# Another order for the first tiles of a fused conv, scan and FFN kernel: one load queue, half of the first u between two v stages, the third x split earlier

## The chip, the cores and the metric

The kernel runs on 1 core of a Trainium2 chip. The metric is the device time of the program in microseconds, as the median of several runs. The engines are TensorE (PE), VectorE (DVE), ScalarE (ACT), GpSimd (POOL) and SyncE (SP, which here only issues DMAs). Each runs its own list of instructions in the order written, and they wait for each other on semaphores.

## The reference

The input x has 8192 rows (tokens) of 512 numbers. Cut to what matters:

```python
def attn(x):                       # called with layernorm(x)
    u, v = split(x @ in_proj_w + in_proj_b, 2)      # 512 -> 2 x 512
    v = conv3_depthwise(silu(v)) + conv_b           # along the tokens
    h_t = a * h_(t-1) + ssm_b * v_t                 # a = sigmoid(logit_a); a scan over the tokens
    y = ssm_c * h + ssm_d * v
    out = (u * silu(y)) @ out_proj_w + out_proj_b
    return layernorm(out + x) * ln_w + ln_b
def ffn(x):                        # called with layernorm(x)
    h = gelu(x @ ternary(W1).T + b1)                # 512 -> 2048
    return h @ ternary(W2).T + b2                   # 2048 -> 512
# ternary(w) = clip(round(w / mean|w|), -1, 1): the threshold needs the whole of w
x = x + layernorm(attn(layernorm(x)))
x = x + layernorm(ffn(layernorm(x)))
```

## The kernel before

The tokens are cut into 16 tiles of 512 (TT), each as four blocks of 128 rows (j) and, transposed, as four blocks of 128 features (b). The stages of a tile are:

- **front**: layer norm statistics of x on DVE (`ln1`: `x_stats`, `aggr`), 1/sqrt on POOL (`rstd_x`), the normed x on ACT (`norm_x`), and its split into two 16-bit halves, `t_hi` on ACT and `t_lo` on DVE, in one of four buffers `tp`. SP then issues one DMA transpose for each block j into `x1T` (`transposes("t1", t)`).
- **v** and **u** (`in_proj`): 12 matmuls of 128x512 for each b. v goes through `silu_v` on ACT, the three conv taps (`centre_tap` on ACT, `taps` first and second on DVE, with the edge column of the next tile copied by POOL), `d_conv` on ACT, `scan` and `y` on DVE, `silu_y` on ACT. `gate` (DVE) multiplies by u; `gate_hi` (ACT) and `gate_lo` (DVE) split the result.
- **o**: the output projection, 48 matmuls, then on DVE `h_add`, `h_stats` and `norms`: `a1`, `a2`, statistics, `x1`, statistics, `n3`, with three 1/sqrt on POOL between them (`rstd`, `rstd_b`, `rstd`). `t_hi` and `t_lo` split the result for the transposes into `x3T` ("t3").
- **f1** and **f2**: 16 blocks j each of 8 matmuls a tile. A block of f1 goes through `gelu` and `hi` on ACT and `lo` on DVE; f2 follows LAG = 4 blocks behind.

The weights are prepared ahead of the tiles. in_proj is scaled by a power of two found from its largest entry and split (`split_in` on ACT, `setup_split` on DVE); out_proj is split too (`split_out`, `setup_out_proj`). For the ternary weights |W1| and |W2| are summed (`abs_sum`, four quarters each, on ACT or DVE), the sum goes across the partitions by a small matmul (`threshold(0)` for W1, `threshold(1)` for W2), and then each weight is turned into -1, 0, 1 by a `sign` on ACT and a `ternary` on DVE, by chunks in the list ORDER. `w_ok` counts the finished chunks. Chunks 16 and up are loaded a second time (`reload(o)`), and their buffers come free as ternaries end: `reload(16)` waits for chunk 12, and so on. `w_ok` 4 releases the first f1, `w_ok` 8 the first gelu (its buffers held raw W1), `w_ok` 12 the first `lo`.

PSUM has eight banks: `misc` 0 and 1 for u, v and o, `f1b` 0 and 1 for f1, `f2b` 0 to 3 for the sums of f2. In the first tiles, where f1 and f2 haven't begun, all eight serve v, u and o (`bank`). From step 2 on `take` lets a group have its `misc` bank when the reader of the group two places ahead in the list `groups` is done: `gate` for a u, `silu_v` for a v, `h_add` for an o.

The order of work of the first tiles is written out by hand on every engine. On TensorE it is v(0), v(1), threshold(0), u(0), the output projection of tile 0 (`o_first`, which takes block k as soon as `gate_lo(0, k)` is done), v(2) with threshold(1) inside it. Then come the steps s = 2, 3, ...: step s does f1 and f2 of tile s-2, u and o of tile s-1 and v of tile s+1. In step 2 nine blocks of f1 come first, with f2 four behind, then u(1), four blocks of f2, o(1), half of v(3), the rest of f1. On DVE, ACT and POOL a step's items are sorted by hand-set times (`AT_...`), and step 2's list for DVE holds the scans and gates of tile 1, the `lo` of the first nine blocks and ternaries 12 to 20 (`AT_TERNARY`). `warm(n)` issues n matmuls of 128x128 in fp32, two instructions each, whose result nobody reads.

SP's order is: x tile 0, in_proj, x tile 1, the transposes of tile 0, the row vectors, out_proj, the transposes of tile 1, x tile 2, W1 quarter 2, W2, the transposes of tile 2, those of x3 of tile 0, then the reloads. W1 quarters 0, 1 and 3 are issued by ACT, after in_proj's third quarter has landed.

## Time and profile before

| | us |
|---|---|
| time before, median of 3 runs | 1496.58 (1496.28 to 1498.77) |
| the profiled execution, its own time | 1500.86 |
| its span | 1498.8 |
| TensorE busy in it | 1421.8 (95%) |
| DVE, ACT, POOL busy | 1117.8, 862.3, 426.1 |
| TensorE's first matmul of v(0) | 28.75 |
| first matmul of o(0), of v(2), of f1(0, 0) | 68.22, 105.01, 117.29 |
| first matmul of o(1) | 171.46 |

The span is the time between the first and the last recorded instruction; the execution's own time is some 2 us longer. All times of the profile are counted from the start of the span. A timeline row is a start, a duration, the engine with the line of the kernel, the operation with what it writes and reads, and the count; behind it in brackets is the idle time of the engine just before, with what ended it. A queue row (SPq) is the time that the issue takes, not the transfer.

### The profile page before, as it was taken

To read this page: it belongs to the slowest core of one execution; us is meant where nothing else is said; L and a number is where in the kernel's file an instruction comes from. 1 tells how busy PE (TensorE), PEld (TensorE's weight loads), DVE (VectorE), ACT (ScalarE), POOL (GpSimd) and SP (SyncE) were. 2 spreads that over 40 slices of the span, in tenths; PEclk is the share of its full clock that TensorE was granted. 3 is DMA by queue.
4 is the path that set the end of the run, shared out by engine and by line. 5 is a ranking of instruction groups with operands and counts; after the bars stand their busy time and mean duration, and the time that the engine had idled before them with its cause. 6 is when DMAs were issued, how large, how long until landed. Compare 5 with 4: busy or idle time off the path is not lost. (4 is left out here: it accounts for less than half of the span.)

```text
span 1498.8 us, 18784 instructions
## 1 busy us (share of the span) xinstructions
PE 1421.8 (95%) x6441; PEld 700.4 (47%) x6441; DVE 1117.8 (75%) x1871; ACT 862.3 (58%) x1252; POOL 426.1 (28%) x490
## 2 busy tenths in 40 slices
PE   4937989999999999999999999999999999999997
PEld 2413534545454454544545454454545445455443
DVE  6886688686777968677786867878686787898634
ACT  5645565565665556566555656655565675653543
POOL 2021203233151423315142331414233151422211
PEclk9969999999999999999999999999999999999999
DMA  9332321131131122113121221212122121101200
GB/s 298 124 98 57 92 64 57 29 85 29 29 85 25 61 29 74 39 29 82 23 66 29 68 46 29 78 23 70 29 59 54 29 78 19 45 1 28 57 28 29
DMA packets 160896, 85.13 MB, mean 57 GB/s; under 512 B 137121, under 2 KB 137121, under 8 KB 160673
## 3 DMA queue, kind: packets, MB, share of 16 engines
q1 hardware_dynamic: 159216, 80.79, 21.5%
...
## 5 line engine op out<-in xcount | busy, mean ns | idle before, releaser
L524 PE MATMUL f2b<-w,ring 128*128 128x512 fp8e5 x1008 | 383.4, 380 | 1.1
L525 PE MATMUL f2b<-w,ring 128*128 128x512 fp8e5 x1008 | 382.8, 380 | 0.0
L500 PE MATMUL f1b<-x3T,w 128*128 128x512 f16 x960 | 367.0, 382 | 15.3 <-ACT ring L1074 11.2
L501 PE MATMUL f1b<-x3T,w 128*128 128x512 f16 x960 | 366.8, 382 | 0.0
L1074 ACT ACTIVATE ring<-f1b,par 128x512 f32<-128x512 f32 x256 | 174.8, 683 | 218.9 <-PE f1b L501 218.5
L640 DVE SCALAR_TENSOR_TENSOR ring<-ring,f_sc 128x512 f16<-128x512 f32 x256 | 210.9, 838 | 53.1 <-ACT ring L1082 53.1
L1337 POOL TENSOR_SCALAR ve<-mv 128x4 f32<-128x4 f32 (+1 forms) x82 | 29.0, 353 | 759.7 <-DVE mv L632 759.5
L459 PE MATMUL misc<-x1T,win_hi 128*128 128x512 f16 x472 | 179.8, 381 | 26.6 <-DMA x1T<-tp 25.2
L1082 ACT ACTIVATE ring<-ring,f_sc 128x512 f16<-128x512 f32 x256 | 180.2, 710 | 0.0
L460 PE MATMUL misc<-x1T,win_hi 128*128 128x512 f16 x472 | 179.7, 381 | 0.0
L461 PE MATMUL misc<-x1T,win_lo 128*128 128x512 f16 x472 | 179.6, 381 | 0.0
L500 PEld LDWEIGHTS f1b<-x3T,w 128*128 128x128 fp8e5 x960 | 94.3, 98 | 137.4 <-issue 16.2
L524 PEld LDWEIGHTS f2b<-w,ring 128*128 128x128 f16 x1008 | 98.8, 98 | 125.9 <-DVE ring L640 8.0
L525 PEld LDWEIGHTS f2b<-w,ring 128*128 128x128 f16 x1008 | 98.8, 98 | 117.9 <-issue 1.3
L501 PEld LDWEIGHTS f1b<-x3T,w 128*128 128x128 fp8e5 x960 | 94.4, 98 | 112.3 <-issue 2.7
L1166 ACT ACTIVATE vb<-misc,par,inv_sig 128x512 f32<-128x512 f32 x58 | 45.0, 776 | 159.1 <-PE misc L461 159.0
L626 DVE BATCH_NORM_STATS2 bn<-hb 128x6 f32<-128x512 f32 x184 | 119.0, 681 | 0.3
L696 DVE SCALAR_TENSOR_TENSOR vl<-vb,par,vl 128x512 f32<-128x512 f32 x128 | 107.0, 870 | 3.9 <-ACT vl L1102 3.8
L1373 POOL TENSOR_TENSOR hb<-hb,xs 128x512 f32<-128x512 f32 x60 | 101.0, 1711 | 27.2 <-ACT hb L1093 27.2
L1386 POOL TENSOR_TENSOR hb<-hb,row 128x512 f32<-128x512 f32 x60 | 79.8, 1334 | 89.8 <-ACT hb L1123 85.0
L1378 POOL COPY carry<-vl 128x1 f32<-128x1 f32 x60 | 80.7, 1357 | 70.5 <-DVE vl L705 69.2
L470 PE MATMUL misc<-wo_hi,g_hi 128*128 128x512 f32 x240 | 98.1, 409 | 0.7 <-DVE hb L751 0.4
...
## 6 DMA issues: line engine op xcount, KB each, us to landing
out_dram<-hb SPq DMA_DIRECT2D x64, 256.0 KB, 2.0
xs<-x_dram SPq DMA_DIRECT2D x15, 1024.0 KB, 5.4
ring<-w1t_dram ACTq DMA_DIRECT2D x3, 1024.0 KB, 9.3
...
ring<-w2t_dram SPq DMA_DIRECT2D x2, 1024.0 KB, 7.5
x3T<-w2t_dram SPq DMA_DIRECT2D x2, 1024.0 KB, 5.4
ring<-w2t_dram SPq DMA_DIRECT2D x8, 256.0 KB, 2.7
x1T<-tp SPq DMA_TRANSPOSE x68, 3.0
```

The costliest lines, as they stand in the source:

```text
L459: pe.matmul(o[:, :], wh, x1T[:, s_, k, :], start=k == 0, stop=False)
L460: pe.matmul(o[:, :], wh, x1T[:, s_, KC + k, :], start=False, stop=False)
L461: mm = pe.matmul(o[:, :], wl, x1T[:, s_, k, :], start=False, stop=k == KC - 1)
L500: pe.matmul(b[:, :], w, src[:, k, :], start=k == 0, stop=False)
L501: mm = pe.matmul(b[:, :], w, src[:, KC + k, :], start=False, stop=k == KC - 1)
L524: pe.matmul(f2b[q][:, :], h_hi[:, i % H_SLOTS, qs], w2[:, j, :], start=j == 0, stop=False)
L525: mm = pe.matmul(f2b[q][:, :], h_lo[:, i % H_SLOTS, qs], w2[:, j, :], start=False, stop=j == FC - 1)
L626: ve_.bn_stats(raw_stats(ln)[:, j, :], src).then_inc(bn_ok[ln], 1)
L640: ve_.scalar_tensor_tensor(out=h_lo[:, i % H_SLOTS, :], in0=gg[:, i % G_SLOTS, :], scalar=f_sc[:, 0:1], in1=h_hi[:, i % H_SLOTS, :], op0=A ...
L696: ve_.scalar_tensor_tensor(out=dst, in0=src, scalar=w, in1=dst, op0=ALU.mult, op1=ALU.add).then_inc(done, 1)
L1074: act.activation(gg[:, i % G_SLOTS, :], f1b[i % 2][:, :], ACT.Gelu, bias=par[:, B1 + j:B1 + j + 1], scale=1.0 / ACT_SCALE).then_inc(gelu_o ...
L1082: act.activation(h_hi[:, i % H_SLOTS, :], gg[:, i % G_SLOTS, :], ACT.Copy, scale=f_sc[:, 0:1]).then_inc(hh_ok, 1)
```

## The change

- **Loads.** ACT issues no loads any more. SP issues all, in the order: as before up to the transposes of tile 0, then out_proj, the row vectors, W1 quarter 0, x tile 2, W1 quarter 1, the transposes of tile 1, W1 quarters 3 and 2, two quarters of W2, the transposes of tile 2, the other two of W2, the transposes of x3. The threshold sum takes W1 quarters 3 and 2 on ACT and 0 and 1 on DVE (before: 0 and 1 on ACT, 3 and 2 on DVE).
- **TensorE.** The order is v(0), two blocks of u(0), v(1), one block of u(0), threshold(0), the last block of u(0), the output projection, v(2), two blocks of u(1), threshold(1), 24 warm rounds, step 2 with the other two blocks of u(1). 16 warm rounds stand ahead of v(0). The banks of the first tiles are dealt out anew.
- **Third x tile.** Its statistics, front, `t_lo` and transposes come ahead of the first output projection's end; its normed x goes to `yb`.
- **First layer norms.** The norms of tile 0 are done for blocks 0 and 1 and then 2 and 3, kind by kind, with 1/sqrt on POOL for each pair (`half_ok`). The ternaries of chunks 0 to 11 all come after the last `t_lo` of x3, and those of 12 to 15 right behind `lo(0, 0)`.

The diff, cut to its core (blank lines and most context left out):

```diff
-AT_TERNARY = {12: 1.5, 13: 2.5, 14: 3.25, 15: 3.7, 16: 4.4, 17: 5.4, 18: 5.6, 19: 6.6, 20: 7.5,
+AT_TERNARY = {12: 1.21, 13: 1.22, 14: 1.23, 15: 1.24, 16: 4.4, 17: 5.4, 18: 5.6, 19: 6.6, 20: 7.5,
...
-        groups = [("v", 2, b) for b in range(KC)]
+        groups = []
...
-            if (kind, t) in (("v", 0), ("u", 0)):
+            if (kind, t) == ("v", 0):
                 return f2b[i]
             if (kind, t) in (("v", 1), ("o", 0)):
-                return (misc + f1b)[i]
+                return (f1b + f2b[:2])[i]
+            if (kind, t) in (("u", 0), ("v", 2)):
+                return (misc + f2b[2:])[i]
             return misc[misc_no[kind, t, i] % 2]
...
-            return (hb, yb)[t][:, j, :] if t < 2 else xn[:, :]
+            return (hb, yb, yb)[t][:, j, :] if t < 3 else xn[:, :]
...
-                    sp.wait_ge(abs_ok[1], 1)
+                    sp.wait_ge(abs_ok[0], 1)
...
             load_x(1)
             transposes("t1", 0)
+            sp.dma_start(wo_raw, w_out_d).then_inc(wout_in, 16)
             sp.dma_start(row[:, :, :], rows.partition_broadcast(P)).then_inc(row_in, 16)
-            sp.dma_start(wo_raw, w_out_d).then_inc(wout_in, 16)
+            load_w1(0)
+            load_x(2)
+            load_w1(1)
             transposes("t1", 1)
-            load_x(2)
-            sp.dma_start(w1_raw[2], w1_d[2]).then_inc(w1_in[2], 16)
+            load_w1(3)
+            load_w1(2)
             load_w2(0, 1, w2_raw[0])
             load_w2(1, 2, w2_raw[1])
+            transposes("t1", 2)
             load_w2(2, 0, w2_raw[0])
             load_w2(3, 3, w2_raw[1])
-            transposes("t1", 2)
             transposes("t3", 0)
...
-                if (kind, t) in (("u", 0), ("o", 0)):
-                    pe.wait_ge(v_ok, i + 1 + (KC if kind == "o" else 0))
+                if (kind, t) == ("v", 1) and i >= 2:
+                    pe.wait_ge(v_ok, i - 1)
+                elif (kind, t) == ("u", 0) and i >= 2:
+                    pe.wait_ge(v_ok, i + 1)
+                elif (kind, t) == ("o", 0):
+                    pe.wait_ge(v_ok, KC + i + 1)
+                elif (kind, t) == ("v", 2):
+                    pe.wait_ge(g_ok, i + 1)
+                if t == 0 or (kind, t) in (("v", 1), ("v", 2)):
...
-                    pe.wait_ge(h_ok, m + 1)
+                    pe.wait_ge(v_ok, 2 * KC + m + 1)
...
+                pe.wait_ge(thr_ok, 2)
...
+                if i < 2:
+                    pe.wait_ge(h_ok, i + 1)
...
+                elif j == 0:
+                    pe.wait_ge(h_ok, NB)
+                    pe.wait_ge(v_ok, 3 * KC)
+                    pe.wait_ge(thr_ok, 4)
...
-                warm(8)
+                warm(6)
...
                 warm(4)
+                pe.wait_ge(x1_lo, 3)
+                warm(16)
...
+                pe.wait_ge(v_ok, KC + 1 if m == 0 else 3 * KC)
...
-            for t in range(2):
-                for b in range(KC):
-                    in_proj("v", t, b, v_mm)
+            for b in range(KC):
+                in_proj("v", 0, b, v_mm)
+            in_proj("u", 0, 0, u_mm)
+            in_proj("u", 0, 1, u_mm)
+            for b in range(KC):
+                in_proj("v", 1, b, v_mm)
+            in_proj("u", 0, 2, u_mm)
             threshold(0)
-            for b in range(KC):
-                if b == KC - 1:
-                    pe.wait_ge(thr_ok, 2)
-                in_proj("u", 0, b, u_mm)
+            in_proj("u", 0, 3, u_mm)
             o_first()
             for b in range(KC):
-                if b == 2:
-                    threshold(1)
                 in_proj("v", 2, b, v_mm)
+            in_proj("u", 1, 0, u_mm)
+            in_proj("u", 1, 1, u_mm)
+            threshold(1)
+            pe.wait_ge(x3_lo, 3)
+            pe.wait_ge(h_ok, 2)
+            warm(24)
...
-                    for b in range(KC):
+                    for b in range(2 if c == 1 else 0, KC):
                         in_proj("u", c, b, u_mm)
...
             setup_in_proj()
+            t_lo("t1", 0, 2)
+            t_lo("t1", 0, 3)
             for k in range(KC):
                 setup_split(k)
+                x_stats(1, k)
+            for j in range(NB):
+                aggr(0, 1, j)
             ffn_scale()
-            for j in range(NB):
-                t_lo("t1", 1, j)
             for k in range(KC):
                 setup_split(KC + k)
-            abs_sum(3)
-            ve_.tensor_scalar(bu_sig[:, :], par[:, BIN:BIN + KC], sig[:, 0:1], None, ALU.mult).then_inc(par_ok, 1)
-            for b in range(KC):
-                taps(0, b, True)
+            setup_scales()
+            setup_out_proj(0)
+            t_lo("t1", 1, 0)
+            setup_out_proj(1)
+            t_lo("t1", 1, 1)
+            setup_out_proj(2)
+            t_lo("t1", 1, 2)
+            setup_out_proj(3)
+            t_lo("t1", 1, 3)
+            run(ln1(2))
+            abs_sum(0)
+            taps(0, 0, True)
+            taps(0, 1, True)
+            abs_sum(1)
+            taps(0, 2, True)
+            taps(0, 3, True)
+            taps(0, 0, False)
+            scan(0, 0)
+            y(0, 0)
+            taps(0, 1, False)
+            threshold_sum(0)
+            scan(0, 1)
+            taps(0, 2, False)
+            y(0, 1)
             ve_.wait_ge(par_ok, 8)
-            taps(0, 0, False)
-            setup_out_proj(0)
-            setup_out_proj(1)
-            taps(0, 1, False)
-            scan(0, 0)
-            abs_sum(2)
-            threshold_sum(0)
-            setup_out_proj(2)
-            setup_out_proj(3)
-            y(0, 0)
-            taps(0, 2, False)
-            scan(0, 1)
-            y(0, 1)
-            threshold(0)
+            gate(0, 0)
+            scan(0, 2)
             taps(0, 3, False)
-            scan(0, 2)
             y(0, 2)
-            gate(0, 0)
-            scan(0, 3)
-            y(0, 3)
             gate_lo(0, 0)
             gate(0, 1)
+            scan(0, 3)
+            threshold(0)
+            y(0, 3)
+            gate_lo(0, 1)
             gate(0, 2)
-            gate_lo(0, 1)
+            gate_lo(0, 2)
+            t_lo("t1", 2, 0)
             gate(0, 3)
-            gate_lo(0, 2)
             gate_lo(0, 3)
-            for o in range(4):
-                ternary(o)
-            for j in range(NB):
-                h_add(0, j)
-                h_stats(0, j)
-            for j in range(NB):
-                aggr(1, 0, j)
-            run(ln1(2))
+            for j in range(1, NB):
+                t_lo("t1", 2, j)
             first = norms(0)
-            run(first[:2 * NB])
-            t_lo("t1", 2, 0)
-            run(first[2 * NB:2 * NB + 2])
-            t_lo("t1", 2, 1)
-            run(first[2 * NB + 2:4 * NB])
-            ternary(4)
-            t_lo("t1", 2, 2)
-            ternary(5)
-            run(first[4 * NB:5 * NB])
-            t_lo("t1", 2, 3)
-            run(first[5 * NB:7 * NB])
-            ternary(6)
-            ternary(7)
+            A1, A2, B_STATS, B_AGGR, X1, C_STATS, C_AGGR, N3 = range(8)
+            def first_norm(kind, js):
+                for j in js:
+                    first[NB * kind + j][1]()
+            pairs = range(0, 2), range(2, 4)
+            for js in pairs:
+                for j in js:
+                    h_add(0, j)
+                    h_stats(0, j)
+                for j in js:
+                    aggr(1, 0, j)
+            for js in pairs:
+                for kind in (A1, A2, B_STATS, B_AGGR):
+                    first_norm(kind, js)
             threshold_sum(1)
-            for j in range(NB):
-                run(first[7 * NB + j:7 * NB + j + 1])
-                if j:
-                    t_lo("t3", 0, j - 1)
-            t_lo("t3", 0, NB - 1)
+            for js in pairs:
+                for kind in (X1, C_STATS, C_AGGR):
+                    first_norm(kind, js)
             threshold(1)
-            for o in range(8, 12):
+            for js in pairs:
+                first_norm(N3, js)
+                for j in js:
+                    t_lo("t3", 0, j)
+            for o in range(12):
...
-                if i > 2 * NB:
+                if n == 2:
+                    act.wait_ge(glo_ok, j + 1)
+                elif i > 3 * NB:
...
-            act.wait_ge(win_in[2], 16)
-            for q in (0, 1, 3):
-                act.dma_start(w1_raw[q], w1_d[q]).then_inc(w1_in[q], 16)
             for j in range(NB):
                 front(0, j)
-            abs_sum(0, 0, w1_raw[0], w1_in[0])
+            for i in range(2 * KC):
+                split_in(i)
             for k in range(KC):
-                split_in(k)
+                split_out(k)
             for j in range(NB):
                 front(1, j)
-            for k in range(KC):
-                split_in(KC + k)
             for b in range(KC):
                 silu_v(0, b)
+                centre_tap(0, b)
+            abs_sum(0, 3, w1_raw[3], w1_in[3])
             silu_v(1, 0)
-            for b in range(KC):
-                centre_tap(0, b)
-            split_out(0)
-            split_out(1)
+            d_conv(0, 0)
             silu_v(1, 1)
-            d_conv(0, 0)
-            split_out(2)
-            split_out(3)
+            abs_sum(1, 2, w1_raw[2], w1_in[2])
+            silu_y(0, 0)
             silu_v(1, 2)
             d_conv(0, 1)
-            abs_sum(1, 1, w1_raw[1], w1_in[1])
-            silu_y(0, 0)
             silu_v(1, 3)
             d_conv(0, 2)
             silu_y(0, 1)
             gate_hi(0, 0)
             d_conv(0, 3)
             silu_y(0, 2)
-            sign_w1(0)
             gate_hi(0, 1)
             silu_y(0, 3)
             gate_hi(0, 2)
+            front(2, 0)
             gate_hi(0, 3)
-            sign_w1(1)
+            for j in range(1, NB):
+                front(2, j)
+            abs_sum(2, 4, w2_raw[0], w2_in[0])
+            abs_sum(3, 5, w2_raw[1], w2_in[1])
             for b in range(KC):
                 centre_tap(1, b)
-            abs_sum(2, 4, w2_raw[0], w2_in[0])
-            abs_sum(3, 5, w2_raw[1], w2_in[1])
-            front(2, 0)
-            front(2, 1)
             abs_sum(4, 6, w2_raw[0], w2_in[2])
-            front(2, 2)
             abs_sum(5, 7, w2_raw[1], w2_in[3])
-            front(2, 3)
+            sign_w1(0)
+            for b in range(KC):
+                silu_v(2, b)
+            sign_w1(1)
             for j in range(NB):
                 t_hi("t3", 0, j)
-            for b in range(KC):
-                silu_v(2, b)
             act.wait_ge(abs_ok[0], 6)
             sign_block(w2[:, 0:4, :], w2_raw[0], w2_in[2], 1)
+            sign_w1(2)
...
-                    items.append((.5, lambda: sign_w1(2)))
...
+            rstd_x(2)
             first_edge(0)
             first_edge(1)
+            keep_state(0, 0)
             first_edge(2)
-            keep_state(0, 0)
+            keep_state(0, 1)
             first_edge(3)
             pool.tensor_copy(v[:, 1, :, 0:1], v[:, 0, :, TT:TT + 1]).then_inc(left_ok, 1)
-            for b in range(1, KC):
-                keep_state(0, b)
-            rstd(1, 0, rsc[:, 0, :], True)
-            rstd_x(2)
-            rstd_b(0)
-            rstd(3, 0, rsc[:, 2, :], True)
+            keep_state(0, 2)
+            keep_state(0, 3)
+            halves = slice(0, 2), slice(2, NB)
+            for i, js in enumerate(halves):
+                rstd(1, 0, rsc[:, 0, js], True, js, (half_ok[1], rs_ok[1])[i])
+            for i, js in enumerate(halves):
+                rstd_b_half(js, (half_ok[2], rs_ok[2])[i])
+            for i, js in enumerate(halves):
+                rstd(3, 0, rsc[:, 2, js], True, js, (half_ok[3], rs_ok[3])[i])
```

## Rows read from the trace of the kernel before

**Rows 1.** The page, busy time of each engine over the span.

```profile
PE 1421.8 (95%) x6441; PEld 700.4 (47%) x6441; DVE 1117.8 (75%) x1871; ACT 862.3 (58%) x1252; POOL 426.1 (28%) x490
```

**Rows 2.** Waits of TensorE, whole span: us in total, times, longest.

```profile
PE misc L459 <- DMA x1T<-tp: 25.2, 1, 25.2
...
PE f1b L500 <- ACT ring L1074: 11.2, 5, 3.7
...
PE f2b L459 <- DMA x1T<-tp: 6.1, 1, 6.1
```

**Rows 3.** Busy time by stretch: length, busy by engine, clock, DMA share, GB/s.

```profile
18.00:20.00 2.00, 2.00 (x11) 2.00 (x11) 1.97 (x5) 1.97 (x4) 0.00 (x0) 1.00 1.05 388
...
28.75:54.90 26.15, 23.24 (x97) 9.86 (x97) 20.12 (x22) 20.91 (x31) 7.39 (x8) 0.89 0.81 237
...
79.80:105.00 25.20, 0.00 (x0) 0.03 (x1) 24.20 (x54) 9.34 (x12) 7.11 (x10) 0.60 0.39 107
...
105.00:117.30 12.30, 12.29 (x51) 5.34 (x52) 5.54 (x12) 4.63 (x7) 1.46 (x2) 0.85 0.45 86
...
117.30:154.40 37.10, 29.23 (x114) 11.62 (x113) 27.00 (x37) 22.77 (x31) 4.42 (x6) 0.86 0.18 56
...
230.00:1450.00 1220.00, 1216.04 (x5556) 600.30 (x5555) 931.25 (x1547) 715.13 (x1046) 379.40 (x411) 1.00 0.19 46
```

**Rows 4.** Timeline of DVE: start, us, line, operation, count, idle before.

```profile
60.16 1.22 DVE L705 TENSOR_TENSOR_SCAN vl<-a_par,vl 128x512 f32<-128x512 f32 x1
...
77.70 0.75 DVE L751 SCALAR_TENSOR_TENSOR hb<-misc,inv_sig,hb 128x512 f32<-128x512 f32 x1 [4.12 <-PE misc L485]
...
109.94 1.47 DVE L744 SCALAR_TENSOR_TENSOR tp<-hb,tp 128x512 f16<-128x512 f32 x2
...
120.27 2.74 DVE L891 SCALAR_TENSOR_TENSOR w<-ring,thr,w 128x512 fp8e5<-128x512 f32 x4 [7.64 <-ACT w L1181]
...
157.24 0.75 DVE L731 SCALAR_TENSOR_TENSOR yb<-misc,bu_sig,yb 128x512 f32<-128x512 f32 x1 [1.98 <-PE misc L461]
```

**Rows 5.** DVE by line from 74 to 112 us: busy, mean ns | idle before.

```profile
L626 DVE BATCH_NORM_STATS2 bn<-xs 128x6 f32<-128x512 f32 x8 | 4.9, 675 | 0.0
...
L891 DVE SCALAR_TENSOR_TENSOR w<-ring,thr,w 128x512 fp8e5<-128x512 f32 x4 | 2.8, 734 | 0.0
...
L744 DVE SCALAR_TENSOR_TENSOR tp<-xn,tp 128x512 f16<-128x512 f32 x4 | 2.8, 689 | 0.8 <-ACT tp L1152 0.8
...
L791 DVE TENSOR_SCALAR hb<-xs,mv,rsc 128x512 f32<-128x512 f32 x4 | 2.1, 543 | 0.9 <-POOL rsc L1338 0.9
```

**Rows 6.** Timeline of ACT.

```profile
64.53 1.99 ACT L1181 ACTIVATE w<-ring,thr 128x2048 fp8e5<-128x2048 f32 x1
...
138.62 1.52 ACT L1190 ACTIVATE w<-xs,thr 128x512 fp8e5<-128x512 f32 x2 [4.65 <-DMA xs<-w2t_dram]
```

**Rows 7.** DMA issues from 0 to 160 us: KB each, median us to landing.

```profile
xs<-x_dram SPq DMA_DIRECT2D x3, 1024.0 KB, 5.8
...
xs<-w2t_dram SPq DMA_DIRECT2D x4, 256.0 KB, 2.6
```

**Rows 8.** Timeline of SP's queue.

```profile
16.07 10.52 SPq L379 DMA_TRANSPOSE x1T<-tp  x4
...
29.55 8.69 SPq L379 DMA_TRANSPOSE x1T<-tp  x4
...
108.58 5.37 SPq L379 DMA_TRANSPOSE x3T<-tp  x4
```

**Rows 9.** Timeline of TensorE, warm rounds.

```profile
16.74 3.55 PE L531 MATMUL f1b<-ones 128*128 128x128 f32 x16 [8.10 <-ACT tp L1152]
...
20.24 1.06 PE L531 MATMUL f1b<-ones 128*128 128x128 f32 x8
```

**Rows 10.** Timeline of POOL (bias adds), and line 837 on DVE (min/median/max ns).

```profile
32.07 6.34 POOL L1386 TENSOR_TENSOR hb<-hb,row 128x512 f32<-128x512 f32 x4 [4.78 <-DMA row<-rows_dram]
...
L837 DVE SCALAR_TENSOR_TENSOR win_lo<-xs,wmax,win_hi x8: 740/750/1758, 24.4 to 38.9; 128x512 f16<-128x512 f32 x8
```

57 lines of the change are left out of this document (31 added, 26 removed).

## The prediction

> **What bounds the kernel now.** I read the page first: TensorE is busy 95% of the span, DVE 75% [rows 1]. So the matmuls set the time, and only what TensorE idles or runs at half speed can be won. The waits say where that is: 25.2 us once for the transposed third x tile, 11.2 us for the GELU, 6.1 us for the first x tile [rows 2]. The stretches place them. From 230 to 1450 us TensorE works 1216 of 1220 us at clock 1.00, so nothing is to be had there; from 79.8 to 105.0 it does nothing, and from 117.3 to 154.4 it works 29.2 of 37.1 us at clock 0.86 [rows 3]. So the change must win ahead of the second output projection, which starts at 171.46 us (TensorE is full from 154.4 to there). Behind that point the work and its order are the same, so the gain is the shift of that point.
>
> In the gap DVE is busy 24.2 of 25.2 us [rows 3]: it carries the layer norms of tile 0, from the first h_add at 77.70 to the last split t_lo, which ends at 111.4 [rows 4], and between them the statistics and the split of x tile 2 and four ternaries [rows 5].
>
> **The change, part by part.** Unit prices: a DVE pass over 128x512 every 0.67 us (four ternaries in 2.74), a scan 1.2 [rows 4], bn_stats 0.61 (eight, back to back, in 4.9 [rows 5]); an ACT pass 0.65, one over 2048 columns 1.9 to 2.0 [rows 6]; 12 matmuls at full speed 2.6 us (0.216 each, 1216 us over 5556 [rows 3]); 1 MB loaded in 2.7 us at 388 GB/s [rows 3], landing 5.8 us after its issue [rows 7].
>
> *Start of TensorE.* Three W1 loads leave ACT's queue, where they ran against the transposes of tile 0: SP issued those four in 10.5 us, but four of x3 in 5.4 when nothing else was loading [rows 8]. ACT issues nothing now and starts its fronts as soon as POOL has the scales, some 4 us earlier. w_in is reduced by 14.7, its reciprocal comes at 17.1, the last t_lo ends at 18.4, the last transpose lands near 23. The 16 warm rounds (32 matmuls at 0.14 us, as the second row of [rows 9]) fill 17.8 to 22.5. So v(0) starts at 23, not at 28.75, and at full speed. By itself this is worth nothing: v(0), two u blocks, v(1) and two more u blocks take 31 us, wait some 2 us for tile 1, and end near 57; then the output projection waits for DVE.
>
> *The DVE and ACT chain to the first output projection.* SP now issues w_out, row and W1(0) at 21 to 22.5, x(2) and W1(1) at 27 (they wait for win_l 8, the last split of w_in), then tile 1's transposes, then W1(3) and W1(2). On ACT split_out waits for w_out until 26, front(1) ends at 34. POOL's bias adds (four in 6.34 us [rows 10]) now lie over DVE's four t_lo and four setup_out_proj; I give those 1.0 us each. So the last t_lo of tile 1 ends at 36.5 and its transposes land at 41, behind the rest of x(2) and W1(1). W1(3) lands at 45; ACT's abs_sum takes it to 47, and only then comes silu_v(1,0), 47.7. That releases the edge copy, taps(0,0) and d_conv(0,0), and scan(0,0) starts at 49.3. From here DVE and ACT hand over to each other: scan(0,1) 54.0 (ACT has abs_sum(1), silu_y, silu_v and d_conv first), scan(0,2) 57.2, scan(0,3) 61.0, threshold(0) 62.5, last gate_lo 69. The projection waits for thr_ok, so it starts at 62.5, 5.8 us after TensorE's last u block. The gap of before ran 20 of 25 us at half clock (0.60, that is 1.2 GHz for 80%), so the clock fell 5 us into it, and 3.7 us of 105.0 to 117.3 (0.85) were still slow [rows 3]. I charge half clock on 5 us of matmuls, 2.5 us. Four groups of 2.8 us: the end is 76.3, the first h_add 74.4 against 77.70. Gain **3.3 us**; bounds 6 (no half clock) and -3 (loads 6 us later than placed here).
>
> The Trainium skill (SBUF — State Buffer, "Who interferes with whom") says that a DVE instruction with two SBUF inputs and a GpSimd one that reads SBUF block each other for their whole length. The trace agrees in its longest case: a win_lo split beside the bias adds took 1.76 us, the median is 0.75 [rows 10]. By the rule alone each of the eight passes could wait out one bias add, and the last t_lo of tile 1 would come some 2 us later; the sum has 1.0 us each, between the two rows.
>
> *From the first h_add to the last t_lo of x3.* Before: 33.7 us. Taken out: four bn_stats and aggregates of tile 2, 2.7; its four t_lo, 2.8, with 0.8 us of waits for ACT; four ternaries, 2.8; the 0.9 us wait for POOL's rstd ahead of n3 [rows 5] (each pair's rstd is now hidden by the other pair's passes, 4 us against some 2 on POOL; without that cover the three would cost 1 to 2 us each). Put in: threshold(1), 0.4, and hand-overs inside the pairs, 0.7. That is 10.0 less and 1.1 more: 24.8 us, the chain ends at 99.2. Gain **8.9**; bounds 6 and 10. Tile 2's split now lies ahead of the projection's end: front(2) on ACT ends at 72.5, the last t_lo at 73.2, the transposes land at 76.5, so v(2) follows the projection at once. Behind it u(1,0) waits for silu_v(2,0) at 87.4 (ACT has four abs_sums, four centre taps and sign_w1(0) first; the last abs_sum waits for a load that lands at 82.7), and u(1,1) ends near 92.7.
>
> *From there to f1(0,0).* Before 117.3 less 111.4, 5.9 us, TensorE being busy with v(2). After, TensorE idles from 92.8; at 98.6 x3_lo 3 releases 24 warm rounds, 48 matmuls. At the 0.22 us of the first row of [rows 9] they take 10.6 us, at the 0.14 of the second 6.9. The clock will have fallen and takes 4 to 6 us to come back, so I take 8.6: f1 starts at 107.2, though the x3 transposes land near 103.5. Cost 8.0 against 5.9: **-2.1**; bounds -4.1 and -0.4.
>
> *From f1(0,0) to the second output projection.* Before 117.3 to 171.46, 54.2 us. The matmuls in it (9 f1, 9 f2, 4 u blocks) are 41.4 us at full speed; 12.8 were stalls and half clock. Most of that came from ACT, whose sign of a reloaded chunk waited for its DMA (4.65 us in the row of [rows 6]) and held the GELU; the reloads in turn wait for ternaries 12 to 15, which were spread through DVE's list. Now the four stand right behind lo(0,0), and a reload lands 2.6 us after its issue [rows 7]: chunks 16 to 19 are there by 119, ACT needs them from 118. The 12.8 go. Two of the four u blocks are gone too, 5.2 us (they ran in the gap). New: u(1,2) needs the bank that gate(1,0) reads, and the gate, which before waited 1.98 us for TensorE [rows 4], stands at the end of DVE's list. lo(0,0) starts at 112.1; 28 passes of 0.67 and 4 scans of 1.2 follow and the gate ends at 136.3. TensorE has nothing from 132.0 on (f2(0,4) too waited 0.5 for ternary 16): stall **4.9**. 54.2 - 12.8 - 5.2 + 4.9 + 0.2 = 41.3. Gain **12.9**; bounds 9 (DVE 4 us later) and 16 (its list faster, the stall half as long).
>
> Sum: 3.3 + 8.9 - 2.1 + 12.9 = **23.0 us**: the second output projection starts at 148.5 instead of 171.46. The profiled execution took 1500.86 us (span 1498.8), 4.3 above the median of the runs, 1496.58. Taken from the median: **1474 us**; the span of a profile like that of before would be 1476.
>
> **Rivals.**
> *Loads too late in one queue.* Some 11 MB of loads and tile 1's transposes go through SP in order. The mechanism: tile 1's four transposes land at 44 to 46 and not at 41, W1(3) and W1(2) follow 4 to 7 us later, and abs_sum holds silu_v(1,0) in ACT's order, so the chain to the projection slips as much. For it: tile 1's transposes took 8.7 us to issue among 2 MB [rows 8]. Against: half of that is in my 41. 23 - 7 = 16, 1481 us. The Trainium skill (DMA: Bandwidth & Descriptors, "Queues, rings and completion order") speaks for it: each DMA engine takes a ring's descriptors in order, so in one queue a transpose stands behind every load issued before it, where two queues would take turns.
> *Step 2 keeps its pace.* What DVE wins in the norms it gives back in step 2: twelve ternaries (8 us) now stand between the last t_lo and lo(0,0), and if ACT or POOL add waits to its list, u(1,2) waits longer, so the 12.9 shrinks to 3: 1484 us. Against: DVE had 10 us of waits in 117.3 to 154.4 (27.0 busy of 37.1 [rows 3]) to fill.
> *Small terms.* No half clock at either place, f1 at 105, the gate earlier: 28 us, 1468.
> *Slower.* abs_sum(0,3) stands ahead of silu_v(1,0) on ACT. If W1(3) landed after 68 instead of 45, the 23 us would be gone and the kernel slower. That needs the 5 MB ahead of it to run at some 130 GB/s; [rows 3] shows 388 in one stretch and 237 over 26 us.
>
> **Chances.** Forecast (1469 to 1479) 0.62; loads late 0.13; step 2 keeps its pace 0.09; small terms 0.11; slower 0.03, no change 0.02. The likeliest one's own range is 1469 to 1479; taken out to the others it is 1466 to 1484. Under 0.2% (3 us) a difference of this kernel can't be told from none. Faster 0.95, same 0.02, slower 0.03.
>
> **What the profile after would show.** v(0) at 23; TensorE idle ahead of the projection, 57 to 62.5; the 25.2 us wait for x1T gone; first h_add 74.4, last t_lo of x3 99; warm rounds to 107; a wait of TensorE for the gate of some 4 us ending near 136; the second projection at 148.5; no long ACT wait for reloads ahead of it. The prediction would be wrong if W1(3) landed after 50, if the wait for the gate passed 8 us, or if the later stalls (the last GELU and x3T waits of [rows 2]'s kind, near 200 and 222) grew.

## The result, and the profile after

The kernel after the change took 1481.11 us (median of 4 runs, 1479.76 to 1484.24) against 1496.82 us (4 runs, 1496.28 to 1498.77) for the kernel before in the same comparison: ratio 0.9896, 95% interval 0.9876 to 0.9915. It is 15.7 us faster, where 22.6 were forecast (1496.58 to 1474). The profiled execution took 1479.76 us, its span 1477.6.

The page's busy times of the kernel after, as in [rows 1]: TensorE's share rose to 97%, with 76 more instructions, all of them of the warm rounds, and 4.6 us more of busy time.

```profile
PE 1426.4 (97%) x6517; PEld 710.7 (48%) x6517; DVE 1118.1 (76%) x1871; ACT 862.8 (58%) x1252; POOL 405.7 (27%) x497
```

Waits of TensorE after, as in [rows 2].

```profile
...
PE misc L481 <- DVE yb L764: 5.4, 2, 4.0
PE f1b L525 <- DMA x3T<-tp: 5.0, 3, 3.8
PE f1b L560 <- DVE tp L777: 4.9, 1, 4.9
PE f1b L481 <- DMA x1T<-tp: 4.2, 1, 4.2
...
PE f1b L506 <- DVE thr L912: 2.6, 1, 2.6
PE f1b L525 <- ACT ring L1120: 2.0, 1, 2.0
```

The 25.2 us for the third x tile of [rows 2] are gone, and all but 2.0 of the 11.2 for the GELU. In their place stand 4.2 us for tile 1, 2.6 for the threshold, 4.9 ahead of the warm rounds and 4.0 for the gate.

Stretches after, as in [rows 3]: v(0) to v(1), v(2) to the warm rounds, f1(0,0) to o(1), and the steady part.

```profile
23.59:43.53 19.94, 15.70 (x72) 6.97 (x73) 17.87 (x34) 14.85 (x21) 9.92 (x10) 0.97 1.04 315
79.00:100.60 21.60, 15.96 (x74) 7.25 (x75) 20.49 (x45) 15.38 (x19) 10.01 (x16) 1.00 0.31 104
107.58:150.22 42.64, 38.09 (x170) 16.65 (x168) 35.52 (x55) 28.19 (x44) 19.15 (x10) 0.96 0.24 74
230.00:1450.00 1220.00, 1215.26 (x5555) 600.04 (x5553) 915.45 (x1532) 706.12 (x1033) 335.82 (x401) 1.00 0.19 45
```

Where before 25 us of the norms left TensorE empty, it now works 16.0 of 21.6 us, and DVE is still full (20.5 of 21.6). The steady part is the same. Milestones, forecast beside two profiled executions of each kernel (the second ones are experiments 1 and 2):

| | before | again | forecast | after | again |
|---|---|---|---|---|---|
| v(0) | 28.75 | 27.09 | 23 | 23.59 | 23.22 |
| first h_add | 77.70 | 76.24 | 74.4 | 75.67 | 74.93 |
| last t_lo of x3 ends | 111.41 | 109.96 | 99.2 | 101.14 | 100.96 |
| f1(0,0) | 117.29 | 115.88 | 107.2 | 107.58 | 107.89 |
| o(1) | 171.46 | 170.19 | 148.5 | 150.22 | 151.43 |
| o(1) to the end of the span | 1327.3 | 1326.2 | same | 1327.4 | 1326.6 |

The last line places the whole gain ahead of o(1): 21.2 us in the first pair of profiles, 18.8 in the second.

DVE after, as in [rows 4]: the first h_add, the last t_lo of x3, the ternaries in one block, the gate of tile 1, and the statistics of x tile 3.

```profile
75.67 0.75 DVE L784 SCALAR_TENSOR_TENSOR hb<-f1b,inv_sig,hb 128x512 f32<-128x512 f32 x1 [0.19 <-PE f1b L508]
...
99.85 1.29 DVE L777 SCALAR_TENSOR_TENSOR tp<-hb,tp 128x512 f16<-128x512 f32 x2 [0.24 <-ACT tp L1200]
101.06 8.03 DVE L926 SCALAR_TENSOR_TENSOR w<-ring,thr,w 128x512 fp8e5<-128x512 f32 x12
...
135.82 1.40 DVE L764 SCALAR_TENSOR_TENSOR yb<-misc,bu_sig,yb 128x512 f32<-128x512 f32 x2
138.49 2.47 DVE L659 BATCH_NORM_STATS2 bn<-xs 128x6 f32<-128x512 f32 x4 [1.26 <-DMA xs<-x_dram]
```

DVE from 74 to 102 us after, grouped as in [rows 5]: neither group now waits for POOL, and n3 (L828) took 2.0 us with no idle time before it, where [rows 5] had 0.9.

```profile
L804 DVE SCALAR_TENSOR_TENSOR hb<-hb,mv,row 128x512 f32<-128x512 f32 x4 | 2.8, 731 | 0.0
...
L828 DVE TENSOR_SCALAR hb<-xs,mv,rsc 128x512 f32<-128x512 f32 x4 | 2.0, 542 | 0.0
```

POOL's bias adds and DVE under them after, as in [rows 10]; then ACT and SP's queue, as in [rows 6, 8].

```profile
30.77 6.30 POOL L1432 TENSOR_TENSOR hb<-hb,row 128x512 f32<-128x512 f32 x4 [3.38 <-DMA row<-rows_dram]
```

```profile
30.96 1.62 DVE L777 SCALAR_TENSOR_TENSOR tp<-yb,tp 128x512 f16<-128x512 f32 x1 [1.90 <-ACT tp L1200]
32.51 1.76 DVE L899 TENSOR_TENSOR wo_lo<-x3T,wo_hi 128x512 fp32r<-128x512 f32 x1
34.19 1.76 DVE L777 SCALAR_TENSOR_TENSOR tp<-yb,tp 128x512 f16<-128x512 f32 x1
35.87 1.75 DVE L899 TENSOR_TENSOR wo_lo<-x3T,wo_hi 128x512 fp32r<-128x512 f32 x1
37.55 0.68 DVE L777 SCALAR_TENSOR_TENSOR tp<-yb,tp 128x512 f16<-128x512 f32 x1
```

```profile
27.37 2.20 ACT L1252 ACTIVATE wo_hi<-x3T 128x512 fp32r<-128x512 f32 x4 [4.26 <-DMA x3T<-w_out_dram]
29.47 0.80 ACT L1190 ACTIVATE yb<-xs,nm,rs 128x512 f32<-128x512 f32 x1
...
46.93 1.91 ACT L1224 ACTIVATE w<-ring 128x2048 fp8e5<-128x2048 f32 x1 [4.42 <-DMA ring<-w1t_dram]
```

```profile
14.49 6.94 SPq L392 DMA_TRANSPOSE x1T<-tp  x4
21.47 0.58 SPq L406 DMA_DIRECT2D x3T<-w_out_dram  x1
...
32.62 8.72 SPq L392 DMA_TRANSPOSE x1T<-tp  x4
...
133.28 0.38 SPq L338 DMA_DIRECT2D xs<-x_dram  x1
```

While POOL adds (30.8 to 37.1), each DVE pass lasts 1.62 to 1.76 us, as long as one bias add (6.30 over four) and a little; behind it, 0.68. And ACT waits 4.42 us for W1 quarter 3 ahead of silu_v(1,0), as the forecast said, but to 46.9 and not to 45.

### The profile page after: what moved, and what is told of

It is laid out like the page before. It is cut to its first block and busy times, and to the rows that moved or that the text cites. A ratio compares the mean times of both kernels' runs of the same rounds, so it can differ in the third digit from the quotient of the medians.

```text
span 1477.6 us, 18945 instructions
## 1 busy us (share of the span) xinstructions
PE 1426.4 (97%) x6517; PEld 710.7 (48%) x6517; DVE 1118.1 (76%) x1871; ACT 862.8 (58%) x1252; POOL 405.7 (27%) x497
## 5 line engine op out<-in xcount | busy, mean ns | idle before, releaser
L673 DVE SCALAR_TENSOR_TENSOR ring<-ring,f_sc 128x512 f16<-128x512 f32 x256 | 208.6, 828 | 47.7 <-ACT ring L1128 47.7
L1378 POOL TENSOR_SCALAR ve<-mv 128x4 f32<-128x4 f32 (+2 forms) x85 | 30.1, 354 | 776.5 <-DVE mv L665 776.3
L481 PE MATMUL misc<-x1T,win_hi 128*128 128x512 f16 x464 | 176.8, 381 | 7.4 <-DVE yb L764 5.4
L482 PE MATMUL misc<-x1T,win_hi 128*128 128x512 f16 x464 | 176.6, 381 | 0.0
L483 PE MATMUL misc<-x1T,win_lo 128*128 128x512 f16 x464 | 176.4, 380 | 0.0
L1216 ACT ACTIVATE vb<-misc,par,inv_sig 128x512 f32<-128x512 f32 x54 | 41.8, 776 | 151.6 <-PE misc L483 151.5
L494 PE MATMUL misc<-wo_hi,g_lo 128*128 128x512 f32 x240 | 95.0, 396 | 0.0
```

Of the source, the lines that this page charges most:

```text
L481: pe.matmul(o[:, :], wh, x1T[:, s_, k, :], start=k == 0, stop=False)
L482: pe.matmul(o[:, :], wh, x1T[:, s_, KC + k, :], start=False, stop=False)
L483: mm = pe.matmul(o[:, :], wl, x1T[:, s_, k, :], start=False, stop=k == KC - 1)
L673: ve_.scalar_tensor_tensor(out=h_lo[:, i % H_SLOTS, :], in0=gg[:, i % G_SLOTS, :], scalar=f_sc[:, 0:1], in1=h_hi[:, i % H_SLOTS, :], op0=A ...
```

## The experiments

Ratios are to the kernel before, measured beside each. Diffs are against the kernel after, cut to their core.

**1 and 2. Each kernel once more.** The profiled execution of before had taken 1500.86 us, 4.3 above its median, and that of after was the shortest of its runs. How much of the 21.2 us is chance?

> The kernel before, unchanged, for a second profile. Theory A: the first profile of before was an execution with much half clock (5 stretches between 54 and 228 us), 4.3 us above the median, and a part of the 21 us by which the second output projection moved was that half clock. Then this execution, if it is near 1496.6, has the second output projection 2 to 5 us ahead of 171.46, with fewer us of half clock between 54 and 172. Theory B: the time is lost or won elsewhere: the projection starts at 171.5 again, whatever the execution took.

> The changed kernel, unchanged, for a second profile and a tighter ratio. Theory A: 0.9896 again within 0.002; and in an execution of about 1482 the second output projection starts 1 to 4 us behind 150.2, by half-clock stretches that the first profile did not have. Theory B: it starts at 150.2 and the time is lost behind it.

Before again: 1498.3 us. After again: 1481.57 us (1479.83 to 1482.89), ratio 0.9889 (0.9869 to 0.9908). The milestones are in the table. In before, TensorE's clock is at its lower level (1.2 GHz) in the same six stretches up to 230 us both times, with lengths that agree within half a us, most of them some 1.4 us earlier the second time, as v(0) is (1.66). So half clock does not explain the difference of these two executions. Of the 2.4 us between their spans 1.3 are there at o(1): in_proj landed earlier (ACT, which waits for its third quarter, issues W1 at 10.76 and not at 12.26). The other 1.1 lie behind it, where the last GELU wait is 1.39 us and not 3.32, and the next wait for x3T 3.79 and not 2.97. In after, the stretch at u(1,2) lasted 3.4 us once (137.9 to 141.3) and 6.8 us the other time (135.4 to 142.2, the first 1.5 of them idle), and f1(0,0) to o(1) took 42.6 and 43.5 us.

**3. Bias adds later.** The passes under POOL's bias adds took 1.75 us, not the 1.0 of the sum.

```
+            rstd_x(2)
             for j in range(NB):
                 add_bias(0, j)
-            rstd_x(2)
```

> The changed kernel with POOL's four bias adds behind the scale of the third x tile instead of ahead of it, so that they no longer lie over the t_lo of the second tile and the split of out_proj. Theory A (two SBUF inputs on DVE block against POOL's reads): the four DVE passes that took 1.6 to 1.8 us take 0.7, the last t_lo of the second tile ends at 35.6 instead of 39.4, its transposes land 3 us earlier, the wait of TensorE for them shrinks from 4.2 to 1 to 2 us, and the first h_add comes 1 to 3 us ahead of 75.7; the kernel is 1 to 3 us faster. Rival (the transposes stand behind the loads in the one queue): the passes are short, but the transposes still land at 43 and nothing moves.

1480.27 us (1479.06 to 1483.21), ratio 0.9883 (0.9858 to 0.9908). DVE and the wait for tile 1 in that run:

```profile
32.19 0.69 DVE L777 SCALAR_TENSOR_TENSOR tp<-yb,tp 128x512 f16<-128x512 f32 x1
32.79 0.69 DVE L899 TENSOR_TENSOR wo_lo<-x3T,wo_hi 128x512 fp32r<-128x512 f32 x1
...
34.92 0.69 DVE L777 SCALAR_TENSOR_TENSOR tp<-yb,tp 128x512 f16<-128x512 f32 x1
```

```profile
PE f1b L481 <- DMA x1T<-tp: 4.8, 1, 4.8
```

Every pass took 0.69 us, and the last t_lo of tile 1 ended at 35.6 instead of 39.4. Yet TensorE waited as long: SP spent 10.18 us on the four transposes, from 31.54, against 8.72 from 32.62. They stand behind x(2) and W1(1) in the one queue. One by one, the issues follow each other without a gap, and the second alone takes 3.75 us:

```profile
35.23 3.75 SPq L392 DMA_TRANSPOSE x1T<-tp  x1
```

The doubled passes were real and cost nothing here, because the queue was the later of the two.

**4. f2 ahead of u(1,2), u(1,3).** This takes away the wait for the gate.

```
+                if s == 2:
+                    for f in left:
+                        f()
                 if c is not None and s < NT:
                     for b in range(2 if c == 1 else 0, KC):
                         in_proj("u", c, b, u_mm)
-                for f in left:
-                    f()
+                if s != 2:
+                    for f in left:
+                        f()
```

> The changed kernel with TensorE's four waiting f2 blocks of step 2 ahead of the other two u blocks. Theory A: the 4.0 us wait of u(1,2) for the gate goes, because the lo blocks are there from 132.6 on; the second output projection starts 3 to 4 us earlier, 146 to 147; the kernel is 3 to 4 us faster. Rival: the f2 blocks wait for lo and ternaries nearly as long, or the gates of the last two u blocks, now right ahead of the projection, bring the wait back there: under 1 us.

1483.46 us (1482.97 to 1483.59), ratio 0.9901 (0.9884 to 0.9919). The wait is gone and o(1) starts at 145.46, 4.8 us earlier than in after, but then stands:

```profile
PE misc L492 <- DVE hb L788: 6.9, 1, 6.9
```

The last block of o(1) ends at 166.5 against 162.3. The stall only moved.

**5. Third x split late.** The statistics of x tile 2, its front, its t_lo and its transposes go back behind the projection; the 24 warm rounds are left out. With them go back `silu_v` of v(2) behind t_hi on ACT and threshold(1) behind the last t_lo on DVE (not shown in the cut).

```
-            transposes("t1", 2)
             load_w2(2, 0, w2_raw[0])
             load_w2(3, 3, w2_raw[1])
+            transposes("t1", 2)
...
-            warm(24)
...
-            t_lo("t1", 2, 0)
...
+                t_lo("t1", 2, js[0])
```

> The changed kernel with the third x tile split behind the first output projection again, as before the change: its statistics ahead of a1, its t_lo in between the norms, its front on ACT and its transposes behind the last W2 loads; threshold(1) behind the last t_lo, no 24 warm rounds. If the early split carries the norms' gain (5.4 of 8.9 us forecast, plus the two u blocks that can't run in the gap then, 5.2, and half clock), the last t_lo of x3 comes 5 to 7 us later than the 101 of the changed kernel, TensorE waits 20 us or more in one piece for the third x tile, and the kernel is 8 to 13 us slower than the changed one, 1490 to 1495. Rival (the pairs, the ternaries and the loads carry it): under 4 us slower.

1495.08 us (1493.59 to 1497.11), ratio 0.9979 (0.9969 to 0.9989). The wait is back:

```profile
PE misc L481 <- DMA x1T<-tp: 22.4, 1, 22.4
```

The last t_lo of x3 ends at 109.9, f1(0,0) starts at 124.5, o(1) at 168.8. (That execution began late: its v(0) starts at 25.62, where after has 23.59.) Without the early split only 3.1 us of the gain is left (0.21% of 1498).

**6. Norms not in pairs.** All four blocks of the first norms go through each operation together, with one rstd each.

```
-            pairs = range(0, 2), range(2, 4)
+            pairs = (range(0, 4),)
...
-                rstd(1, 0, rsc[:, 0, js], True, js, (half_ok[1], rs_ok[1])[i])
...
+            rstd(1, 0, rsc[:, 0, :], True)
...
```

> The changed kernel with the norms of tile 0 done for all four blocks at once, 1/sqrt on POOL for all four. Forecast had about 1 us for the wait ahead of n3 that the pairs hide; without them each of the three 1/sqrt on POOL has no DVE work beside it but the threshold steps, so the last t_lo of x3 comes 2 to 6 us later (1.3, 2.4 and 1.7 us of POOL, plus hand-overs) and the kernel is 2 to 6 us slower. Rival: under 1 us, the POOL times are hidden anyway.

1486.01 us (1484.59 to 1486.92), ratio 0.9924 (0.9907 to 0.9940), 4 to 5 us slower than after (by the ratios and by the medians). DVE by line, 74 to 110 us, of that run:

```profile
L802 DVE SCALAR_TENSOR_TENSOR hb<-hb,mv,row 128x512 f32<-128x512 f32 x4 | 2.7, 748 | 1.5 <-POOL rsc L1379 1.5
L817 DVE SCALAR_TENSOR_TENSOR xs<-hb,rsc,xs 128x512 f32<-128x512 f32 x4 | 2.7, 746 | 1.7 <-POOL c L1395 1.7
...
L826 DVE TENSOR_SCALAR hb<-xs,mv,rsc 128x512 f32<-128x512 f32 x4 | 2.1, 541 | 1.3 <-POOL rsc L1379 1.3
```

The three POOL steps show as 1.5, 1.7 and 1.3 us of DVE's idle time, 4.5 in all, within the 1 to 2 us each of the forecast.

**7. Ternaries 12 to 15 spread again** through DVE's list of step 2.

```
-AT_TERNARY = {12: 1.21, 13: 1.22, 14: 1.23, 15: 1.24,
+AT_TERNARY = {12: 1.5, 13: 2.5, 14: 3.25, 15: 3.7,
```

> The changed kernel with ternaries 12 to 15 at their old places in DVE's list of step 2. Theory: the reloads of chunks 16 to 19 are again released late, ACT's signs wait for their DMA and hold the GELU, so TensorE waits again for ring (GELU) 5 to 10 us in step 2 and the kernel is 3 to 8 us slower. Rival (DVE's own list is the bound, its length is the same): under 1 us, since the gate comes at the same time.

1487.47 us (1483.74 to 1490.18), ratio 0.9932 (0.9914 to 0.9950), 5 to 6 us slower. The GELU's wait returns, and the same 6 us stand at o(1) (156.12 against 150.22):

```profile
PE f1b L525 <- ACT ring L1120: 7.7, 3, 3.0
```

**8. Tile 1's transposes ahead of x(2)**, the bias adds behind the splits, the statistics of tile 2 and the sums of W1 on ACT later.

```
             load_w1(0)
-            load_x(2)
             load_w1(1)
             transposes("t1", 1)
+            load_x(2)
             load_w1(3)
...
-            abs_sum(0, 3, w1_raw[3], w1_in[3])
             silu_v(1, 0)
-            d_conv(0, 0)
             silu_v(1, 1)
+            abs_sum(0, 3, w1_raw[3], w1_in[3])
+            d_conv(0, 0)
```

> The changed kernel with x tile 2 loaded behind the transposes of tile 1 (W1 quarter 1 ahead of them), the bias adds on POOL behind the last t_lo of tile 1, the statistics and scale of tile 2 later, and ACT's sums behind the silu of tile 1. Theory (one queue: the transposes of tile 1 stood behind x(2) and W1(1)): the transposes land at 38 to 40 instead of 43.5, TensorE waits under 1.5 us for them, the first output projection starts 2 to 4 us earlier and the kernel is 2 to 4 us faster than the changed one. Rival (from silu_v(1,0) on, DVE and ACT are bound by W1(3) and W1(2) for threshold(0)): the transposes come earlier but the projection does not.

1480.35 us (1476.21 to 1482.74), ratio 0.9883 (0.9865 to 0.9902). v(1) starts at 41.31 instead of 43.53, but scan(0,0) only at 51.02 (51.59), since DVE now waits 3.08 us for x(2); the wait for the threshold grows from 2.6 to 6.1 us, and the first h_add comes at 75.14. The late transposes were worth half a microsecond at h_add, and nothing that the times can tell.

**9. W1 quarters 0, 1 and 3 issued by ACT again.** The forecast called the earlier start "by itself worth nothing".

```
-            load_w1(0)
             load_x(2)
-            load_w1(1)
             transposes("t1", 1)
-            load_w1(3)
...
+            act.wait_ge(win_in[2], 16)
+            for q in (0, 1, 3):
+                act.dma_start(w1_raw[q], w1_d[q]).then_inc(w1_in[q], 16)
             for j in range(NB):
                 front(0, j)
```

> The kernel after, but ACT issues W1 quarters 0, 1 and 3 as in the kernel before (behind in_proj's third quarter), and SP only the rest. My reading, as in the prediction (the start of TensorE is worth nothing by itself): v(0) starts near 28 instead of 23.2 to 23.6, v(1) within 2 us of 43.5, the first h_add between 75 and 77.5, o(1) between 149.5 and 152, time 1480 to 1483. Rival: the earlier start is carried through, so it is lost here as 4 us: the first h_add near 79.5 and 1485. Second rival: with two queues the transposes of tile 1 no longer stand behind the loads, v(1) is not late, and the time is 1478 or less.

1484.69 us (1482.79 to 1485.31), ratio 0.9907 (0.9892 to 0.9922): my expectation failed, the first rival held, with a little less than its 4 us. Experiments 10 and 11, measured beside it, took 1480.53 and 1481.53; by the ratios the loss against after is 1.6 to 2.7 us, by the medians 3.6, and the intervals of the two ratios overlap. v(0) starts at 27.53 and every milestone is late by 3 to 5 us: first h_add 78.59, f1 111.64, o(1) 155.16. SP's queue and ACT of that run:

```profile
15.22 10.20 SPq L392 DMA_TRANSPOSE x1T<-tp  x4
25.46 0.58 SPq L406 DMA_DIRECT2D x3T<-w_out_dram  x1
```

```profile
31.63 2.19 ACT L1249 ACTIVATE wo_hi<-x3T 128x512 fp32r<-128x512 f32 x4 [5.62 <-DMA x3T<-w_out_dram]
33.73 0.80 ACT L1187 ACTIVATE yb<-xs,nm,rs 128x512 f32<-128x512 f32 x1
```

SP issues w_out behind the transposes of tile 0, at 25.46 instead of 21.47; ACT has split_out ahead of front(1), so front(1) starts at 33.73 instead of 29.47, and all of tile 1 with it.

Why are the transposes of tile 0 done 4.0 us later? It is for the most part not the W1 loads beside them. A row of four runs from the start of the first issue to the end of the last, with SP's waits for each t_lo in it. Taken one by one, three of the four take 1.3 to 1.4 us and one 2.34, and after has 1.23 to 1.37. What is late is the start. ACT, which has to wait for in_proj's third quarter before it may issue the loads, begins front(0) at 12.99 instead of 9.42:

```profile
12.99 0.81 ACT L1187 ACTIVATE hb<-xs,nm,rs 128x512 f32<-128x512 f32 x1 [10.37 <-issue]
```

```profile
9.42 0.81 ACT L1190 ACTIVATE hb<-xs,nm,rs 128x512 f32<-128x512 f32 x1 [6.78 <-POOL nm L1390]
```

TensorE's first warm rounds wait for ACT's second t_hi, the transpose of in_proj's maximum stands behind them, and DVE waits for that with the second t_lo of tile 0 behind it (19.27 instead of 15.70):

```profile
PE f1b L557 <- ACT tp L1197: 7.1, 1, 7.1
```

```profile
19.07 0.28 DVE L851 TENSOR_REDUCE wrow<-f2b 1x1 f32<-1x128 f32 x1 [3.88 <-PE f2b L564]
```

The third t_lo is 2.9 us late by this, and the slow issue adds 1.1.

**10. No warm rounds ahead of f1(0,0).**

```
-            warm(24)
```

> The kernel after without the 24 warm rounds ahead of f1(0,0). My reading: DVE's list sets step 2, so TensorE's slow start costs nothing there: f1(0,0) starts near 105.5 at half clock, u(1,2) still starts within 1 us of 136.6 to 136.9, time 1480.5 to 1483. Rival: the rounds are worth what they cost, the first five f1 blocks at half clock come late to the GELU and the lo, and all moves 2 to 4 us: 1484 to 1486.

1480.53 us (1479.36 to 1481.67), ratio 0.9881 (0.9866 to 0.9896): the same as after. The stretch of f1's first 39 recorded matmuls:

```profile
105.72:116.92 11.20, 11.20 (x39) 4.46 (x40) 8.37 (x14) 5.86 (x8) 0.00 (x0) 0.75 0.09 18
```

f1 starts 1.9 us earlier, at half clock for its first 13 matmuls, and has done its first five blocks at 117.14, where after has 116.21. u(1,2) starts at 137.55 (136.62), o(1) at 151.15, within what two executions of after differ. As expected, the rounds are worth nothing here: DVE's list sets step 2.

**11. Gates early.** gate(1,0) and gate(1,1) go ahead of the last lo and ternary of DVE's list of step 2, the four silu_y of tile 1 ahead of the ninth GELU.

```
                 if s == 2:
                     items += [(AT_TERNARY[o], lambda o=o: ternary(o)) for o in FIRST]
+                    items += [(6.65, lambda: gate(c, 0)), (6.66, lambda: gate(c, 1))]
...
-                if c is not None and c > 0:
+                if c is not None and c > 0 and s > 2:
                     gate(c, 0)
                     gate(c, 1)
...
+                    items += [(7.9, lambda b=b: silu_y(c, b)) for b in range(KC)]
```

> The kernel after with gate(1,0) and gate(1,1) moved up in DVE's list of step 2 (ahead of the last lo and the last ternary of the list) and the four silu_y of tile 1 ahead of the ninth GELU on ACT. My reading: the wait of u(1,2) for the gate (4.0 us) goes, with half or all of the half clock behind it; o(1) starts near 146; ACT's fronts and residuals of 145.1 to 154 begin some 3 us earlier with it, so that h_add(1,0) is not late as it was with f2 first; 3 us are kept: 1478. Rival: as with f2 first the stall only moves behind o(1)'s second block (a wait of TensorE for h_add of 4 us or more): 1481 to 1483.

1481.53 us (1480.77 to 1483.5), ratio 0.9886 (0.9870 to 0.9903): nothing kept; the rival held. The wait for the gate fell to 1.3 us and o(1) starts at 147.04, then:

```profile
PE misc L492 <- DVE hb L784: 3.9, 1, 3.9
```

DVE in that run, the statistics of x tile 3 and the first h_add of tile 1:

```profile
139.59 2.47 DVE L659 BATCH_NORM_STATS2 bn<-xs 128x6 f32<-128x512 f32 x4 [1.21 <-DMA xs<-x_dram]
...
156.10 0.74 DVE L784 SCALAR_TENSOR_TENSOR hb<-misc,inv_sig,hb 128x512 f32<-128x512 f32 x1
```

h_add(1,0) comes at 156.10, where after has it at 155.81. This execution was 1.2 us late at f1(0,0) already. Counted from there, h_add(1,0) comes 47.4 us later against 48.2 and 49.1 in the two profiles of after, and o(1) ends 55.6 us later against 54.9 and 55.8. So early gates bring h_add forward by 1 to 2 us at most, and the end of o(1) not at all.

**12. 11 and 8 together.**

> The gates early and also the order of e8 (x tile 2 behind tile 1's transposes, bias adds behind the splits of tile 1, statistics of tile 2 and the two sums of W1 on ACT later). If the two add up: first h_add 75.1, o(1) near 145.5, 1477. If the first is worth nothing, the same as the gates alone. Rival: 1481, both only move stalls.

1479.85 us (1478.36 to 1480.93), ratio 0.9876 (0.9861 to 0.9891). o(1) starts at 145.31, and stands 3.9 us for h_add. It is the lowest median, and its ratio is 0.0020 and 0.0013 below the two of after, 2 to 3 us, with intervals that overlap: it can't be told from no change.

## Why the prediction was right, and where its sizes were off

**The place and the mechanism held, the size was too large.** The time of 1481.1 lies 2 us above the forecast's own range (1469 to 1479) and inside the outer one (1466 to 1484). It is also the 1481 of the rival of loads too late; that is luck, as the first step below shows. The bound was where the forecast read it: the 25.2 us wait came from the late split of x tile 2, and undoing that part alone (experiment 5) gives back 12 to 14 of the 15.7 us (the difference of the ratios and of the medians; with the split went the rounds and the order of a few items around it). Behind o(1) nothing changed (1327.3 and 1327.4 us). None of the signs of being wrong came: W1(3) landed at 46.9 (limit 50), the wait for the gate was 4.0 us (limit 8), and the later waits for the GELU and x3T were 2.05 and 3.76 us, where before had 3.32 and 2.97. The block of ternaries is worth 5 to 6 us (7), the pairs 4 to 5 (6), the W1 loads in SP's queue 2 to 4 (9). With the 12 to 14 these sum to 23 to 29, more than the whole, so they are not terms of a sum. That each exposes a part of the same waits is the plain reading; no two were undone together to show it.

**Term by term**, in the first pair of profiles: the first h_add gained 2.0 us (forecast 3.3), the norms 8.2 (8.9), up to f1(0,0) -0.6 (-2.1), f1(0,0) to o(1) 11.5 (12.9). Sum 21.2 where 23.0 were forecast.

*First h_add.* Each of the steps was late by one to three us: last t_lo of tile 1 at 39.4 (36.5), tile 1's transposes 43.5 (41), W1(3) 46.9 (45), silu_v(1,0) 48.85 (47.7), scan(0,0) 51.6 (49.3), threshold 64.5 (62.5). So the rival of loads too late in one queue was partly true in its places and wrong in its price: it set 7 us on it, and 1.3 were lost in all (2.0 in the second pair). The projection itself started 2.3 us late, at 64.77 (62.5), and won 1.0 back, mostly since 3.7 us of it were at half clock and not the 5 of the forecast. Experiment 3 takes the doubled DVE passes out and 8 the queue's order, and neither gives more than 0.5 us at h_add. The Trainium skill (SBUF — State Buffer, "Who interferes with whom") agrees with the rows: passes of 1.62 to 1.76 us beside bias adds, 0.69 without them. The weighing in the forecast took 1.0 us, and the rule's own reading, a bias add for each pass, was the nearer one for as long as POOL added; by experiment 3 it did not matter for the end. The Trainium skill's rule on order in one queue (DMA: Bandwidth & Descriptors, "Queues, rings and completion order") agrees too: in experiment 3, with the splits 3.8 us earlier, the transposes behind the loads were no earlier. Experiment 9, with W1 in ACT's queue, shows the other bound. Its row for tile 1's transposes is as long, 9.33 us, but the loads ahead had mostly landed (110 GB/s in that stretch, 278 in experiment 3), and one by one they took 1.24 to 1.33 us (in experiment 3 up to 3.75), each right behind its t_lo, and it was the passes doubled by the bias adds that kept SP waiting:

```profile
39.31 1.24 SPq L392 DMA_TRANSPOSE x1T<-tp  x1
```

So two things hold tile 1 back, the loads ahead of it in the queue and the doubled passes, and removing either one leaves the other. To take both away at once, with ACT issuing W1 only after its front(0), was not tried; experiment 8 moved the bias adds and x tile 2 and brought v(1) 2.2 us forward, and then stood for x tile 2.

*"By itself this is worth nothing"* was wrong. The sum held the earlier w_out (split_out waits until 26), but the sentence looked only at TensorE's start. The same step that starts v(0) early, ACT's front(0) without a wait for the loads ahead of it, also ends the transposes of tile 0 and so brings w_out 4 us earlier, and experiment 9 loses 3 to 4 us at the first h_add and 2 to 4 us of time without it.

*Norms.* Rightly sized (8.2 and 7.7, forecast 8.9); the three waits for POOL that the pairs hide are the 1.5, 1.7 and 1.3 us of experiment 6.

*Up to f1.* 48 warm matmuls took 7.14 us, 0.149 each (7.6 in the second profile), near the lower of the two rows; 8.6 had been taken. Experiment 10 shows that this term is no cost at all: without the rounds o(1) starts no earlier.

*f1 to o(1).* The wait for the gate came as forecast, 3.99 us ending at 136.6; with the 0.56 for a ternary ahead of it that is 4.6 for the forecast's 4.9, ending at 136.3. So the rival of step 2 keeping its pace failed: the twelve ternaries took their 8.0 us, and the stretch still gained 11.5, not 3. The term that was left out is half clock behind that wait, 3.4 us in one execution and 6.8 in another (5.1 of them at work), which costs 1.7 and 2.6 us and is nearly the whole difference between 41.3 and the 42.6 and 43.5 measured. What it would be worth to remove the wait, the forecast did not ask: nothing (4, 11). DVE comes to h_add(1,0) at 155.8 to 156.1 whether o(1) starts at 150.2 or at 147.0, since x tile 3's statistics wait for its load until 138.5 to 139.6, and gate_lo, ACT's fronts and residuals and the four t_lo follow. SP issues that load at 133.28, when ternary 19 is done (`load_x(3)` waits for `w_ok` 20). That this load is the bound was read from these rows and not tried, and the time from the statistics to h_add(1,0) isn't fixed: 17.3 and 18.1 us in the two profiles of after, 16.5 in experiment 11.

**From the profile to the median** is the weakest step. The forecast took 23.0, read from an execution of 1500.86 us, off a median of 1496.58. The profiles' shifts are 21.2 and 18.8 us; the medians' differences are 15.7, and 18.2 in experiment 2. What moves is largely before: its medians went from 1496.82 to 1499.81, and its clock goes with it. Of 27 later executions of before, the ten with a mean granted clock of 0.984 or more took 1495.4 to 1497.5 us, the twelve with 0.982 or less 1497.4 to 1501.4. The difference in clock, some 0.0025 of 1498 us, is worth 3.7 us (an estimate), which is the distance. Both profiled executions of before (0.981 and 0.982) belong to the second group, so a part of the half clock that the forecast counted as gain is likely missing in a typical execution. Which stretch of half clock the shorter ones lack, no profile shows. The two profiled executions of after were each the shortest of their runs; those of experiments 5, 9, 11 and 12 were the longest of theirs, so that is likely chance. Against the second pair, 4.2 of the 23.0 us were not there at all.
